# Six of the 24 copies that lay out q and k for the first four heads, issued by ScalarE between two of its own copies instead of by the sync engine

## The reference

```
x = x + A(layernorm(x))     # A: retention with 4 heads, chunked, gated, with rotary positions
x = x + F(layernorm(x))     # F: channel mix: sigmoid(xr W_r) * (relu(xk W_k)^2 W_v)
x = x + B(layernorm(x))     # B: attention, 16 heads of 16, 1024 keys, relative bias
x = x + F(layernorm(x))     # the same channel mix and weights again
```

```
q, k, v = x wq + bq, x wk + bk, x wv + bv
attn    = softmax(q k^T / 4 + rel_bias[bucket(key - query)])
out     = (attn v) wo + bo
```

## Time and profile before

| what | value |
|---|---|
| median of three runs | 3088.31 us (3087.98 to 3089.7) |
| the profiled execution | 3088.87 us, of which the span from first to last instruction is 3086.4 us |
| TensorE (PE), matmuls | 2885.0 us busy, 93% of the span |
| VectorE (DVE) | 2045.4 us, 66% |
| ScalarE (ACT) | 1739.7 us, 56% |
| GpSimd (POOL) | 1250.0 us, 41% |
| mean granted clock of TensorE | 0.972 of full speed |
| SP direct moves (L446) | 192 DMAs of 64 KB, issue 0.59 us each |

### The profile page before, as it was taken

The page is one execution under the profiler, slowest core; times in us unless marked ns, Lnnn a source line. Parts: engine busy times, 40 slices in busy tenths (PEclk is TensorE's granted clock), DMA queues, the critical chain, the costliest instruction groups (busy, mean ns, idle before and its releaser), DMA issues.

```text
span 3086.4 us, 51535 instructions
## 1 busy us (share of the span) xinstructions
PE 2885.0 (93%) x18786; PEld 1495.0 (48%) x18786; DVE 2045.4 (66%) x4319; ACT 1739.7 (56%) x3667; POOL 1250.0 (41%) x1764
## 2 busy tenths in 40 slices
PE   5989999899998999989999999999999899998997
PEld 3643356433664336643466434653346533465334
DVE  4469735796457954589545994469934699346982
ACT  2428834388344873448644586436854368543784
POOL 2325533255332543335443354334543345433453
PEclk8979999999999999999999999999999999999999
DMA  6041000510005000140001400023000320003200
GB/s 176 1 105 20 2 1 1 122 30 2 1 13 124 16 2 1 24 114 16 2 1 41 97 16 1 1 62 76 16 1 1 82 56 16 1 1 82 56 2 14
DMA packets 54779, 107.58 MB, mean 35 GB/s; under 512 B 12400, under 2 KB 34976, under 8 KB 54400
## 3 DMA queue, kind: packets, MB, share of 16 engines
q1 hardware_dynamic: 54528, 104.29, 14.6%
HBM read 56.66 MB, written 36.72 MB: 30 GB/s over the span
## 4 chain that ended last, share of the span: by engine, by line
PE 71%; DVE 13%; SPq 4%; POOL 3%; issue 3%; DMA 3%; ACT 2%; POOLq 0%; DVEq 0%; ACTq 0%
PE psum L736 18%; PE psum L785 16%; PE psum L554 10%; DVE mx L1453 7%; PE psum L762 4%; PE psum L836 4%; SPq L446 3%; PE psum L890 2%; PE psum L817 2%; PE psum L874 2%; DMA parts<-mixed 2%; PE psum L625 2%; PE psum L589 2%; PE psum L893 2%; POOL X L1559 1%
## 5 line engine op out<-in xcount | busy, mean ns | idle before, releaser
L1453 DVE TENSOR_REDUCE mx<-psum 128x1 f32<-128x512 f32 x2048 | 1261.7, 683 | 119.9 <-PE psum L736 119.2
L1196 ACT ACTIVATE Z<-psum 128x512 f32<-128x512 f32 x2048 | 1120.5, 597 | 272.5 <-PE psum L762 240.3
L1649 POOL TENSOR_TENSOR Z<-Z,band_exp 128x256 f32<-128x256 f32 (+1 forms) x1152 | 711.3, 640 | 733.5 <-ACT Z L1196 726.3
L736 PE MATMUL psum<-SK,SQ 63*128 63x512 f32 x2048 | 803.4, 478 | 69.1 <-DVE mx L1453 43.9
L762 PE MATMUL psum<-SQ,SK 64*128 64x512 f32 x2048 | 789.5, 464 | 4.6 <-DMA SQ<-mrow 4.5
L785 PE MATMUL psum<-Z,Vx 128*17 128x256 f32 x8192 | 641.3, 387 | 0.1
L736 PEld LDWEIGHTS psum<-SK,SQ 63*128 63x128 f32 x2048 | 330.6, 192 | 525.0 <-DVE mx L1453 394.2
L554 PE MATMUL psum<-Wqkvg,Z 128*128 128x512 f32 x768 | 368.0, 605 | 1.0 <-ACT Z L1094 1.0
L762 PEld LDWEIGHTS psum<-SQ,SK 64*128 64x128 f32 x2048 | 324.0, 189 | 74.2 <-ACT Z L1196 55.8
L785 PEld LDWEIGHTS psum<-Z,Vx 128*17 128x17 f32 x8192 | 138.4, 95 | 355.1 <-issue 292.0
L1594 POOL TENSOR_TENSOR Z<-Z 128x512 f32<-128x512 f32 x64 | 81.1, 1267 | 304.0 <-DVE Z L1375 304.0
(11 more groups left out here) (121 smaller groups left out, 3269.6 us busy)
## 6 DMA issues: line engine op xcount, KB each, us to landing
parts<-Z SPq DMA_DIRECT2D x32, 512.0 KB
X<-L_attn_a_x SPq DMA_DIRECT2D x8, 1024.0 KB, 5.5
SQ<-parts SPq DMA_DIRECT2D x32, 256.0 KB, 7.5
SK<-parts SPq DMA_DIRECT2D x32, 256.0 KB, 10.6
SQ<-parts SPq DMA_DIRECT2D x16, 512.0 KB, 7.7
SK<-parts SPq DMA_DIRECT2D x16, 512.0 KB, 13.8
out<-X SPq DMA_DIRECT2D x16, 512.0 KB, 19.5
SQ<-mixed SPq DMA_DIRECT2D x96, 64.0 KB, 2.3
```

The source lines that it names most:

```text
L736: pe.matmul(row_bank(c), SQ[rows_of(h, MAX_ROW), h // 2, i * P:i * P + P], SK[rows_of(h, MAX_ROW), h // 2, 512 * k:512 * k + 512], start=T ...
L1196: nc.scalar.activation(ring[:, n % RING, :], col_bank(n), ACT.Exp)\
L1453: nc.vector.tensor_reduce(mx2[:, blk % 2, col, k:k + 1], row_bank(2 * u + k), AX_X, ALU.max)\
L1649: nc.gpsimd.tensor_tensor(ring[:, n % RING, a:z], ring[:, n % RING, a:z], band_exp[:, 4 * hg + COLS[i], at:at + z - a], ALU.mult)\
```

## The change

`spread_directly` now takes the issuing engine and a list of heads. SP issues the 12 moves of q and the six of k for heads 0 and 1. The six of k for heads 2 and 3 are issued by ScalarE, after its copy of v for tokens 512 to 767 (`v_copies(2)`) and ahead of its copy for the last quarter (`v_copies(3)`). The moves themselves, their semaphore and all waits for them stay as they are; ScalarE's list gains the wait for `c_lo`, which the moves of k have always had.

```diff
+        def spread_directly(eng, b, s, heads):
+            need(eng, c_lo, b, 3 + s)
+            stack = (SQ_words, SK_words)[s]
+            for h in heads:
+                for group, part in enumerate(((1, 0, 0), (0, 1, 0))[s]):
+                    r0 = HALF * (h % 2) + HD * group
+                    eng.dma_start(stack[r0:r0 + HD, h // 2, :],
+                                  split[0][s][HD * h:HD * h + HD, part, :].bitcast(F32))\
+                        .then_inc(spread_first[s].sem, 16)
...
-            def spread_directly(b, s):
-                need(sp, c_lo, b, 3 + s)
-                stack = (SQ_words, SK_words)[s]
-                for h in range(4):
...
             for b in range(B):
-                for s in range(2):
-                    spread_directly(b, s)
+                spread_directly(sp, b, 0, (0, 1, 2, 3))
+                spread_directly(sp, b, 1, (0, 1))
...
                 v_copies(2)
+                spread_directly(act, b, 1, (2, 3))
                 v_copies(3)
```

## The result

| | median us | lowest to highest |
|---|---|---|
| before | 3089.7 | 3087.98 to 3091.29, 5 runs |
| changed | 3101.55 | 3100.89 to 3105.54, 5 runs |

The ratio of the two, taken over all runs, is 1.0041, with a 95% interval from 1.0026 to 1.0056: the changed kernel is slower by 0.4%, some 12 us, where 3061 us had been forecast. Its profiled execution took 3100.89 us, with a span of 3099.1 us and a mean granted clock of 0.967.

What follows compares the result with a forecast made beforehand. SP's DMA issuing between projections and attention was taken to bound the kernel. A gain of 3.8 us less 0.4 for traffic, 3.4 in each of 8 batches, took 27 us off 3088.31: 3061 us, range 3056 to 3086.

Steps and rivals of the forecast that it cites:

- What bounds the kernel: Between projections and attention, SP's DMA issuing was said to hold up TensorE; issuing and landing together 5% of the chain.
- Both ways to TensorE: SP's issuing delays TensorE through the direct moves (first score row) and through stores queued behind them (relus, tanhs, transposes).
- Part 1: SP's list six moves shorter: stores of q, relus and possible transposes 3.8 us earlier in each batch.
- Part 2: ScalarE issues six moves of k at 0.63 us each; TensorE's first-row wait shrinks from 2.05 to about 1.1 us.
- Traffic: ScalarE's moves flying beside SP's stores hold the stores up by 0 to 1.9 us; 0.4 us taken.
- The clock: After a first-row gap of 1.1 us TensorE keeps full clock, gaining 3.8 us a batch; otherwise 2.5, total 3067 us.
- Batch 0: First batch, without postponed channel mix: first row 1.7 us earlier, row maxima issued 3.8 us earlier; gain 3.4 us.
- Rival 1: SP and ScalarE take turns issuing DMAs, so transposes come 2.8 us late in seven batches: 3110 us, chance 0.12.
- Rival 2: No gain: ScalarE's issues slow or held by SP's stores of k, or stores fly longer; 3085 us, chance 0.16.

Runs made afterwards that it cites:

- e4: Changed kernel with ScalarE's same six moves of k issued earlier, between projection pieces and after the third copy of v, ahead of the stores: 3071.61 us.
- e8: Kernel before, all moves on SP, with only the two stores of q for heads 4 to 7 made wide (64 plain rows): 3069.06 us.
- e6: e4 with the two stores of q for heads 4 to 7 made wide, in a scratch of their own: 3041.48 us.
- e5: Changed kernel, but SP issues all four stores of heads 4 to 7 only when all moves of k have landed: 3101.06 us.
- e3: Changed kernel with the scratch laid out so that all stores are wide, with six loads back instead of four: 3138.41 us.
- e10: e5 with the two stores of q for heads 4 to 7 made wide: 3050.8 us.
- e7: Changed kernel with ScalarE issuing only the three moves of k of head 3, SP the other nine of k: 3083.66 us.
- e1: Changed kernel with SP issuing all moves, the two stores of q still ahead of the last six moves of k: 3113.84 us.
- e2: Changed kernel, but SP issues the two stores of k only when all moves of k have landed: 3098.67 us.

## Why the prediction was wrong

**What bounds the kernel** was read rightly. Both ways to TensorE are real: e4 takes away the first, e8 the second, and each gains 15 to 20 us; e6 takes both, 47 us. One total was misread: the longest wait for the tanhs, 3.3 us, isn't that of the channel mix that stands alone (0.8) but occurs in batches 3 and 6; the other five have the 1.6 to 1.7 of batch 1. Nothing in the sum hung on it.

**Part 1** came true. The stores were brought forward and the relus start 3.3 us earlier, against 3.8 less 0.4 forecast. The second store of q took 8.6 us (549.9 to 558.5) instead of 8.07, so the 0.4 us allowed for traffic on the stores was about right. It brought nothing, because the other way had become the longer.

**Part 2 is the step that failed**: a pitch of 0.63 us and a landing of 2.46 us after the last issue. Both were rows of the kernel before, where the moves stood ahead of every store. The change itself put the last three of them behind the stores. Measured were issues of 1.17 and 1.92 us and landings of 5.1 and 6.4 us. The last issue started at 551.40, 3.7 us after the first (3.15 forecast), and the first row came 6.5 us after it. In e5, where no store flies beside them, the forecast's own numbers nearly come out: 3.2 us from the first issue to the last, and the first row 2.4 us after it. That the last copy of v would be delayed 0.9 us and stay hidden: it was delayed by about 2.2 (553.36, and 551.2 without the issues) and stayed hidden only because the first row was later still.

**Traffic** was where this should have been seen. I asked what moves do to stores, and not what stores do to moves. The row was there: a store on a quarter of the engines for 8 us. A move spreads its 16 rows over all engines and has landed only with the last of them. So a few busy engines are enough to make it late, however idle the other twelve are: the nine late rows above ran among the packets of the stores, at a DMA share of 0.26. Behind wide stores it is late by less (2.59 in e3).

The Trainium skill, "DMA: Bandwidth & Descriptors", section "Why a DMA increments its semaphore by 16 and not by 1", says that such a DMA uses as many engines as the largest number up to 16 that divides the slowest dimension of both its sides: 4 for these stores, 16 for the moves. The trace agrees, with a share of 0.26 while only stores fly, and so does the shorter flight of e8's stores, whose slowest dimension is 64.

**The clock.** I had bet on full clock after a wait of 1.1 us. e5 and e10, with 0.5 us, do keep it there, and so does e7 with 1.47 us (its first L610 took 1.99). The changed kernel waited 5.08 and ran at half clock for 6.8 us instead of 3.4.

**Batch 0** was to gain 3.4 us and gained 0.8. Its first row, too, came 2.75 us later, and the row maxima were issued 2.0 us later, not 3.8 earlier. What did come true is that their flight shortens: in the kernel before TensorE waited 4.07 us for them at its first product of L762, at 225.17, and in the changed kernel it starts there at 222.38 without that wait. Of the 2.8 us 0.8 is the earlier start of the batch, and of the rest 0.8 was left at its end.

**Rival 1** had the sign, and its 3110 us is nearer than my 3061, but not the mechanism. While SP and ScalarE were both issuing moves (547.73 to 549.2), an issue took 0.52 to 0.63 us on either engine; they didn't take turns. And e1 has the delay with one issuer, e2 a held issue with nobody else issuing. The sign that I had named for it, issues of 1.2 us or more and a first wait above 2, was seen, but it is a sign of other causes too. The Trainium skill, "Perfetto Trace Analysis", section "DMA Instruction — HWDGE (DVE, Sync)", has the shared and locked block that stood behind this rival. With two engines issuing side by side at their usual pitch, such a block can have been locked for at most half of the 0.6 us at a time (an estimate from these issues). I gave Rival 1 0.12 and the forecast 0.72, and no case at all to a move that lands late because of stores.

**Rival 2** was half right: the last issues were held. It put this down to SP's pushing of the stores of k, while e2 has it without those stores; it saw no late landing; and it priced it at 3077 to 3093, little more than the loss of the gain.

What stays open: at which point a held issue waits (all that the runs show is that it comes with DMA engines that are busy); why the narrow stores are slow at first, 59 GB/s; and the 48.9 us of e3.

## What to carry to other kernels

Here a transfer over all DMA engines landed only when its last rows had passed the few engines that other transfers kept busy. So ask of each one that is moved not only who issues it but which transfers are now issued ahead of it, and whether one of them occupies few engines for long. A landing time read from a trace holds for the neighbours it had there. Before shortening a queue, look whether what moves up will collide with what was taken out; here issuing the moves first (e4), or making the stores of q wide and keeping all of them apart from the moves (e10), turned 12 us lost into 15 and 36 us gained, and both measures together (wide stores of q behind early moves, e6) into 47.

## What I had not expected of the hardware

- ScalarE's DMA issue starts 0.01 us after the copy ahead of it has started (547.72 and 547.73), not after it: the queue's issue lies beside the engine's work. An issue takes 0.51 to 0.62 us, like SP's 0.59.
- An issue can be held up while other transfers are in flight: 1.9 us on ScalarE, also with no other engine issuing (e2), 2.1 on SP (e1), and 1.27 with moves alone at a DMA share of 0.97 (e7).
- A move that is issued just ahead of a store is hardly hurt by it: 2.3 to 2.5 us to landing in the kernel before, where the first store follows the last move by 0.63 us, against 3.7 to 7.2 for one issued behind it.
- The same gap of about 2 us at the first row cost 3.4 us of half clock in batch 1 of before, and none in batch 1 of e8 (L621 at 1.99 us). What TensorE had done ahead of it was the same in both lists.
